# Output stage of a cross-attention and mixture-of-experts layer: the eight loads of expert weights move from SyncE's queue to ScalarE's

## The reference, cut to what matters

```python
# x (32, 56, 512), ctx_4096 (32, 1500, 512); 16 heads, 4 key/value heads, head size 96
x = x + attention(layernorm(x), ctx_4096, Wq, Wk, Wv, Wo)     # out @ Wo.T closes it

h = layernorm(x)                                              # here: per token, over D = 512
logits = h @ W_gate + b_gate                                  # 8 experts
_, top_idx = top_k(logits, 2)
y_all = relu(einsum('bsd,edh->bseh', h, W_e) + b_e)
x = x + take_along_axis(y_all, top_idx[..., None], axis=2).mean(axis=2)
```

## Time and profile before

| | |
|---|---|
| median of three runs | 3384.92 us (3384.07 to 3386.4) |
| profiled execution, span from the first to the last instruction | 3388.4 us |
| mean granted TensorE clock | 0.994 of full speed |
| VectorE, ScalarE, GpSimd busy | 61%, 49%, 31% of the span |
| DMA, mean over the span | 84 GB/s |

### The profile page before, as it was taken

How to read it: one execution, slowest core, us unless ns; L and a number is a source line. 1 busy time by engine, 2 the same in 40 slices (tenths; PEclk the granted TensorE clock), 3 DMA queues, 4 the chain that set the end, 5 groups by cost and what they waited for, 6 DMA issues and landing times. The chain is left out here.

```text
span 3388.4 us, 64330 instructions
## 1 busy us (share of the span) xinstructions
PE 3341.6 (99%) x21610; PEld 3107.7 (92%) x21610; DVE 2052.6 (61%) x2995; ACT 1648.8 (49%) x3146; POOL 1051.4 (31%) x865
## 2 busy tenths in 40 slices
PE   8999999999999999999999999999999999998989
PEld 8989999999999999999999999999999999997777
DVE  5346666666666666666666666666666666665645
ACT  3225555555555555555555555555555555552232
POOL 0032223332333333332222222233323333326554
PEclk9999999999999999999999999999999999999989
DMA  6542222222212122222222222222222121226865
GB/s 229 198 144 59 59 65 65 65 61 61 63 46 60 56 63 65 64 65 64 65 65 59 65 57 60 65 65 65 61 61 61 47 61 55 63 75 164 195 194 188
DMA packets 307512, 282.96 MB, mean 84 GB/s; under 512 B 200634, under 2 KB 257546, under 8 KB 307338
## 3 DMA queue, kind: packets, MB, share of 16 engines
q1 hardware_dynamic: 301738, 266.10, 27.6%
q0 software_dynamic: 5728, 16.27, 1.5%
HBM read 208.33 MB, written 73.96 MB: 83 GB/s over the span
## 5 line engine op out<-in xcount | busy, mean ns | idle before, releaser
L822 PE MATMUL ps_proj<-wv_hi,parts 128*125 128x384 f32 x3072 | 875.6, 339 | 0.0
L767 DVE TENSOR_TENSOR probs_lo<-probs,probs_hi 125x448 fp32r<-125x448 f32 (+1 forms) x896 | 682.0, 778 | 275.7 <-ACT probs_hi L694 263.2
L809 PE MATMUL ps_proj<-parts,wk_hi 128*128 128x500 f32 x2304 | 711.1, 390 | 2.9 <-DVEq L722 2.9
L822 PEld LDWEIGHTS ps_proj<-wv_hi,parts 128*125 128x125 f32 x3072 | 560.0, 185 | 5.8
L147 POOL TENSOR_SCALAR parts<-raw 128x1000 fp32r<-128x1000 f32 (+1 forms) x198 | 238.3, 1204 | 957.2 <-PE ps_proj L822 777.8
L686 ACT ACTIVATE probs<-ps_scores 125x448 f32<-125x448 f32 (+1 forms) x896 | 463.0, 517 | 121.6 <-PE ps_scores L870 78.8
L822 PE MATMUL ps_proj<-wv_lo,parts 128*125 128x384 f32 x1536 | 518.4, 338 | 0.0
L809 PEld LDWEIGHTS ps_proj<-parts,wk_hi 128*128 128x128 f32 x2304 | 431.4, 188 | 91.6 <-DVEq L722 3.2
L673 ACT CAST values_hi<-ps_proj 125x384 fp32r<-125x384 f32 x384 | 184.4, 480 | 645.3 <-PE ps_proj L822 645.3
L694 ACT CAST probs_hi<-probs 125x448 fp32r<-125x448 f32 (+1 forms) x896 | 484.1, 540 | 28.3
L736 DVE TENSOR_TENSOR values_lo<-ps_proj,values_hi 125x384 fp32r<-125x384 f32 x384 | 214.3, 558 | 431.6 <-ACT values_hi L673 428.9
(11 more groups left out here) (218 smaller groups left out, 5822.7 us busy)
## 6 DMA issues: line engine op xcount, KB each, us to landing
raw<-in_ctx SPq DMA_DIRECT2D x192, 500.0 KB, 3.6
qk_hi<-proj_out_hi SPq DMA_DIRECT2D x60, 224.0 KB, 2.0
qk_lo<-proj_out_lo SPq DMA_DIRECT2D x60, 224.0 KB, 2.4
queries_hi<-qk_hi SPq DMA_DIRECT2D x32, 336.0 KB, 3.5
queries_lo<-qk_lo SPq DMA_DIRECT2D x32, 336.0 KB, 3.6
att_raw<-attended SPq DMA_DIRECT2D x128, 84.0 KB
probs<-att_raw SPq DMA_DIRECT2D x31, 336.0 KB, 5.7
probs<-inverse_sums SPq DMA_DIRECT2D x31, 336.0 KB, 3.0
```

Of the source, the lines that this page charges most:

```text
L767: dve.tensor_tensor(prs[1][0:R, u % PRING, 0:N], pr[0:R, u % PRING, 0:N], f(prs[0][0:R, u % PRING, 0:N]), ALU.subtract).then_inc(p_lo, 1)
L809: mm = pe.matmul(pproj[n % 2][:, 0:CS], w["wk"][a][:, j // 3, i * P:(i + 1) * P], ct[v][:, c, j // 3, :], start=(j == 0), stop=(j == 3 * K ...
L822: mm = pe.matmul(pproj[n % 2][0:VT, 0:KD], ct[a][:, t // VTC, j // 3, s], w["wv"][v][:, j // 3, :], start=(j == 0), stop=(j == 3 * KT - 1))
```

## The change

ScalarE, not SyncE, issues the eight expert loads, each with the same wait as before. Loads 0 and 1, which have no wait, are issued at the start of ScalarE's list and behind its first split; loads 2 to 7 stand behind the deviation of t = 2, 3, 5, 6, 8 and 9, ahead of ScalarE's split of att(t + 2) and its copy of the transposed rows. Sizes, buffers, semaphores and GpSimd's order are as they were.

```diff
--- before.py
+++ after.py
@@ -1054,12 +1054,6 @@
 
                 def load_x(t):
                     sp.dma_start(x[:, t % 2], x_v[t]).then_inc(g["x_loaded"][t % 2], 16)
-
-                def load_expert(e):
-                    if e >= 2:
-
-                        sp.wait_ge(g["e_lo"], e - 1)
-                    sp.dma_start(w_raw[:, e % 2], io["we"][:, e, 0:EARLY_W]).then_inc(e_loaded[e % 2], 16)
 
                 load(1)
                 load_x(0)
@@ -1086,8 +1080,6 @@
                         store_rows(sp, g, scratch, t - 1)
                     if t == 0:
                         store_att(sp, stream, scratch, B - 1, home)
-                    if t in EXPERT_AT:
-                        load_expert(EXPERT_AT.index(t))
                     if t == OT - 2:
 
                         sp.wait_ge(a_lo, START + OT - 2)
@@ -1186,11 +1178,21 @@
                         act.wait_ge(g["g_done"], t)
                     act.copy(xt[:], pt[:]).then_inc(xt_done, 1)
 
+                def load_expert(e):
+                    if e >= 2:
+
+                        act.wait_ge(g["e_lo"], e - 1)
+                    act.dma_start(w_raw[:, e % 2], io["we"][:, e, 0:EARLY_W]).then_inc(e_loaded[e % 2], 16)
+
                 act.sem_inc(a_hi, 1)
+                load_expert(0)
                 split(1)
+                load_expert(1)
                 act.wait_ge(consts, CONSTS)
                 for t in range(OT - 1):
                     deviation(act, g, t)
+                    if t > 0 and t + 1 in EXPERT_AT:
+                        load_expert(EXPERT_AT.index(t + 1))
                     if t + 2 < OT:
                         split(t + 2)
                     if t < OS:
```

## The result

The changed kernel takes 3402.08 us (median of 5 runs, 3399.2 to 3402.51) where the kernel before, beside it on the same chip, takes 3384.59 (5 runs, 3380.53 to 3386.4): ratio 1.0047, 95% interval 1.0035 to 1.0058. Forecast was 3381.0, with a range to 3391: both the sign and the range were missed. The profiled execution after took 3402.51 us, of which its span is 3400.8; the span before was 3388.4, so the two traces show 12.4 us of the 17.5 between the medians (the trace before was of an execution whose span alone lies 3.8 us above its median). In all other kernels here the time of the profiled execution is 1.7 to 1.9 us above its span, so the trace before is of an execution of about 3390.2 us, an estimate, 5.6 above the median.

A forecast was written before the change was run, and what follows sets the result against it. TensorE, busy 99% of the span, was taken as the bound, losing time to `xn_g` waits. Terms -1.0 - 5.9 + 3.0 = -3.9 us took the span from 3388.4 to 3384.5, 3381.0 unprofiled; range 3374 to 3391.

The forecast's parts named there:

- The price of sharing: Expert weights moving beside the store of xn(t) delay its landing at t = 2, 6 and 8: 1.0 us each, +3.0.
- +18: Upper bound for weights beside stores: weight packets slowed to three times their time by scatters, 6 us on each of three.
- Tile 4: Output stage: store of xn(2) lands in 11.0 us, leaving a wait of 1.3 in place of 7.24: -5.9 us.
- Expert 1 costs nothing: Its load behind ScalarE's first split, at 3072.44, finds the DMA engines nearly idle: no cost.
- Expert 0: Its load at ScalarE's entry, about 3065, meets att(1): cost 0.2 us, taken as 0, bounds 0 and +1.9.
- Tile 2: Store of `xn_g` 0 no longer has expert 0 ahead of it, clearing the transposes' wait: -1.0 us.
- The first scatter: GpSimd splits experts 0 and 1 earlier and reaches its first scatter at about 3092 instead of 3098.75.
- ScalarE's own time: Issuing loads on ScalarE costs 0 if issues stay under 1.7 us; tightest at t = 2, slack 1.71.
- (c): Slower: weight packets in slow stretches hold up stores at norms of tiles 3, 4, 6, 7, 9, 10: +8, 3393; 13%.
- Rival (b): Nothing gained: tile 4 keeps its 7.24 us and sharing eats tile 2's 1.0: 3385; 25%.

The follow-up runs named there:

- experiment 6: All scatters moved behind GpSimd's loop over the splits, in the kernel before and in the changed kernel: 3397.71 and 3402.09 us beside the kernel before at 3391.04.
- experiment 2: Kernel before with only the loads of experts 2 to 7 moved to ScalarE, 0 and 1 staying on SyncE: 3403.15 us beside 3390.48, ratio 1.0035.
- experiment 1: Kernel before with only the loads of experts 0 and 1 moved to ScalarE's queue: 3388.55 us beside 3390.48, ratio 0.9995.
- experiment 5: Kernel before with loads 2 to 7 on ScalarE, issued only once the store of xn(t) has landed: 3392.29 us beside 3383.3, ratio 1.0027.
- `after_late_sc`: Changed kernel with all scatters moved behind GpSimd's loop over the splits: 3402.09 us beside the kernel before at 3391.04, ratio 1.0037.
- `e27_behind`: Kernel before with loads 2 to 7 on ScalarE behind its copy of `xt_g`, some 2 us after the store was issued: 3402.02 us, ratio 1.0033.

## Why the prediction was wrong

The prediction looked in the right place, at the landings of `xn_g`, but of the tiles that it named (4, 6, 8) only tile 4 still waits for one; the others that wait after the change, apart from 0.48 us in tile 2, are 7 and 10 to 12. The steps:

*The price of sharing*, +3.0, is the step that failed. It was set as a sum of small additions: half of a load's 2 us at each of three places. The addition itself is now measured: 2.7 us in the mean (experiment 6), while ScalarE's queue shares and no scatter is about. What it does is not additive: where the store's last packets move from one side of a slow stretch to the other, the landing goes from at most 7.9 to 15.2 us, store 5 of the change. VectorE had no wait at t = 5 before, so I had left that place out, with t = 3 and 9; a place with no wait may be one that just escapes. By itself this half measured +12.7 us (experiment 2). The upper bound I had written, +18, had the right order of size, but not the mechanism. It let packets of weights slow down to three times their time in a scatter's slow stretch. In the changed kernel those of expert 2 kept their time (202 ns in the median after 196) and were through before the slow stretch; what slowed were the packets that they had put off, the stores' among them (353 ns for 2 KB in place of 85).

*Tile 4*, -5.9, did not come. The store of row tile 2 was to meet one pair of scatters and land in 11.0 us. Without a load ahead of it that is near the truth: in experiment 1 it took 12.5 us and tile 4 fell from 17.20 to 11.74, a gain of 5.5. With expert 2's load at 3101.98, ahead of the store at 3103.08, it took 16.9 us. The error is again the load ahead, priced at 1.0 and worth 4.4 here, between one trace of each kernel.

*Expert 1 costs nothing*, since "the DMA engines are nearly idle then", was wrong by 2.7 us in tile 1. I looked at the engines' load in one microsecond and at the transfers that TensorE waits for, not at what SyncE would issue next: a store of 3.5 KB and, behind its landing, the chain to att(2). *Expert 0*, 0, is not contradicted: tile 0, in which it lands, took 10.09 us after 10.96. But no run moves it alone, and line 189 came 1.24 us later, of which tile 0's later start explains 0.85.

*Tile 2*, -1.0: the wait at its transposes fell from 1.00 to 0.48 us, while store 0 was itself later by the start; half right. *The first scatter* came at 3095.61, forecast 3092: the places were late with tile 1. *ScalarE's own time*, 0, was right: all eight issues took 0.33 to 0.39 us, below the 1.7 of slack, and no wait goes back to them.

Of the rivals (c), at 13%, came nearest: the kernel is slower, by stores behind weights, and VectorE's waits stand at the norms of tiles 3, 6, 9 and 10, four of the six that it named (and at 11). It was priced at half of +17; the two medians differ by 17.5, and the six loads alone cost 12.7. How it was to come about, by packets of weights that hold an engine three times as long, is the mechanism of the +18 above, and the trace speaks against it. Its sentence against, that tile 4's own stall would have to stay, was true, and it stayed. Rival (b) had the rule from the same page of the Trainium skill, section "Issuing engines are not separate DMA queues", that issuing from other engines saves only the issuing time. No run shows a saving, which fits with it. But the runs show that the engine of issue sets the order of packets too, and that this was worth 12.7 us the wrong way (experiment 2).

**What stays open.** Why the packets slow down from the moment that a scatter's words travel is not shown; that they don't when the scatters are moved away is (experiment 6). How much of the 9.0 us of experiment 5 comes from ScalarE's own wait, and why a quarter of the bytes is no faster, are open too. Executions in which another store is caught would fit, which one trace for each kernel can't show. The same would explain that the kernel before runs between 3378.68 and 3400.33 us; that was not tested.

## What to carry to other kernels

When a transfer is moved to another queue, price it at the landings it will stand in front of, the small ones and those that had no wait before too, and ask how long the store that frees a buffer may take before somebody waits. If a store's landing is spread widely (here 3 to 19 us) and a single buffer hangs on it, the next microseconds of traffic may cost seven (store 5: at most 7.9, then 15.2 us); a second buffer was worth more than any order tried here (it gained 0.25 to 0.31%, where the wrong order had cost 0.34% and no order gained anything measurable). Before a slow stretch is blamed on an issue, look up when that transfer's own packets travel: for the pairs of scatters above, 6 to 7 us behind the first issue. And a condition that moves one transfer off another has to be checked for what it moves it onto. And keep a load that nobody waits for in the same queue behind the store that somebody does.

## What the runs showed of the hardware

- Twice in the changed kernel (words of a pair of scatters on q0 at 3110.7 to 3112.1 and 3149.6 to 3151.0) 6 to 7 us follow in which the 16 DMA engines are busy (0.82 to 1.19) and move 81 to 94 GB/s, after a stretch of 321 to 365 at about the same share. In the first a packet of 2 KB took 353 ns where it had taken 85. With the scatters away it took 100 in the mean over 3100 to 3180 (`after_late_sc`). It is the tail that they make: the stores of the changed kernel land in 7.7 us in the median with the scatters and in 7.0 without, but singly in 15.2 and 16.9 with them, and in 8.4 at most as long as there are none.
- A load of 655 KB issued from another queue 2.1 us after a store of 256 KB landed with it (landings 13.1 and 15.5 us, 0.3 us apart in time), though its own packets had all begun 5.5 us before (`e27_behind`).
- A load of 655 KB issued 1.7 us ahead of a store of 3.5 KB took the step that waits for its landing from 1.36 to 2.96 us; over the traces of all runs the step took 2.70 to 2.97 us with this load and 1.35 to 1.40 without.
- An issue on ScalarE's queue took 0.33 to 0.39 us, and its record overlaps with the engine's work (both start at 3071.91 and at 3101.98), where SyncE's issues of the same load took 0.43 to 3.16.
